# Early-fusion block on one core: selected rows in two image halves, exponential per image with row sums, residual products among the gather

## The chip, the cores and the metric

The kernel runs on one core of one Trainium2 chip. The metric is the device time of one execution in microseconds (us), lower is better. Runs of the kernel before: 225.53 us median of 3 (224.13 to 226.31).

## The reference

Eight images of 3x128x128 are cut into 64 patches each and embedded in 192 channels (first layer `_L0_tok_ref`: feed-forward, window attention, feed-forward). Each image then gets 32 text tokens, so that 96 tokens per image remain. The middle layer is the one that the change touches:

```python
    qkv = (x @ Wqkv_w + Wqkv_b).reshape(b, l, 3, h, hd)          # h = 12 heads of 16
    scores = jnp.einsum('bthd,bshd->bhts', q, k_ * scale)
    attn = jax.nn.softmax(scores + causal_mask, axis=-1)
    ctx = jnp.einsum('bhts,bshd->bthd', attn, v).reshape(b, l, d)
    attn_output = ctx @ out_w + out_b
    selection = jax.nn.softmax((x @ sel_w + sel_b) / temperature, axis=-1)[..., 1:]
    k_sel = int(math.ceil(math.sqrt(l)))                          # 10 of 96
    _, idx = jax.lax.top_k(selection[..., 0], k_sel)
    gated = attn_output * selection
    src = jnp.take_along_axis(gated, idx[..., None], axis=1)
    y = jax.vmap(lambda xb, ib, sb: xb.at[ib].add(sb))(x, idx, src)
```

Only the 10 picked rows of an image are ever used of the attention, so the kernel computes these alone. With `x` the layer-normed tokens, the block's output is `h + y`; a layer norm of it and a feed-forward layer of 16 gated experts and one shared expert follow (`_L0_ffn_ref`), and they take the rest of the time.

## The kernel before, in words

The program is written out by hand for each engine: PE (TensorE), DVE (VectorE), ACT (ScalarE), POOL (GpSimd) and SP, whose queue issues most transfers. Every engine runs its list in order; what one needs of another is a counting semaphore, `wait_ge(s["name"], n)` before and `.then_inc(s["name"], 1)` behind. So the order of the lines within an engine's block is the order of the work, and there is no planner. Sizes: `TOK` = 96 tokens, `PICKED` = 10, `SLOTS` = 80 picked rows of all images, `HALF_IMG` = 4 images in a half, `H2N` = 384 tokens in a half, `CH` = 96 channels (one of two chunks, `ch`), `CHH` = 6 heads in a chunk, `DIM` = 192, `QROWS` = 124 (60 query rows of chunk 0 from row 0, 60 of chunk 1 from row 64). The eight PSUM banks are `bank[0..7]`.

`keep_busy(site, bank)` (L567) issues `FILL[site]` matmuls on constant data whose result nobody reads; the text calls them fillers.

The stage around the change, in the order of the work, for `hf` = 0, 1 (the two halves):

1. DVE picks the ten best of each image (L1667 to L1683), PE sums ranks (L856), and DVE makes the one-hot matrix `hot` (L1690) and `hotp`, weighted by the selection (L1694).
2. Gather: PE opens two banks with the query bias (L862) and adds 16 small products `qv` x `hot` (8 images x 2 chunks, L870) with one filler before every second; DVE spreads each chunk over its heads into `aq_blk` (L1702).
3. PE turns `hotp` (L875), lays the causal mask into the score banks (8 products, L885), then adds 16 score products (L895).
4. Softmax: per half, DVE takes the maximum of each row and image (`amax`, L1493) and subtracts it (L1495), one ACT instruction takes the exponential of 124x384 (L1293), DVE sums (L1500), inverts (L1502) and multiplies (L1504). DVE does both subtractions first, and then sum, inverse and product of half 0, then of half 1.
5. PE turns the probabilities (L909), ACT moves them to SBUF as `aprobT` (L1296), PE multiplies by the values (16 products, `weighted`, L919).
6. DVE keeps each head's own channels: one product of 96x480 with a 0/1 mask into `actx` (L1724) and two sums over the six heads into `ctxT` (L1730), for each half.
7. PE multiplies the bias rows `avb_all` (L942) and the contexts of all 80 picked rows (L945) by `out_w`; DVE adds `out_b` and writes `arow` (L1735).
8. PE adds the picked rows, through `hotpT` (picks, turned, which DVE makes from bank 7 at L1716), to the residual in four `h2_bank`s (8 products, L953). The residual `hx` itself had been put into these banks earlier by 8 products with the identity (`start_h2`, L902).
9. DVE takes statistics of the sum (L1740, L1745), POOL the inverse root (L447, L449), ACT moves the sum to SBUF as `h2` (L1302), DVE normalises into `xn2` (L1603), PE turns it (L785, L786), and the experts follow.

`down_lo(0, 0)` (L1611) splits the first down-projection's weights on DVE; POOL does the same for the first two up-projections (L516) in the same stretch.

Of the kernel before, what the change touches and what calls it, by code (L numbers as in the profile page):

```python
# [19 lines left out]
ALU = mybir.AluOpType  # L20
# [23 lines left out]
SLOTS = IMAGES * PICKED  # L44
# [42 lines left out]
def build(nc, d):  # L87
    with ExitStack() as ctx:
# [9 lines left out]
        h2_bank = [bank[i] for i in (3, 6, 0, 1)]  # L98
# [127 lines left out]
        with ExitStack() as second_life:  # L226
# [25 lines left out]
            hotpT = sb2("hotpT", [SLOTS, IMAGES, TOK])  # L252
# [5 lines left out]
            actx = sb2("actx", [CH, 2, 2 * HALF_IMG, 60])  # L258
            ctxT = sb2("ctxT", [CH, 2, 2, HALF_IMG * PICKED])
            arow = sb2("arow", [SLOTS, DIM])  # L260
# [20 lines left out]
        def v3(ap, n):  # L281
# [243 lines left out]
        def _(pe):  # L525
# [289 lines left out]
            def keys(hf):  # L815
# [31 lines left out]
            tr(bank[2][0:IMAGES, 0:TOK], psel[:, :], c("ident", TOK)[:, 0:TOK]).then_inc(s["psT_ps"], 1)  # L847
            token_rows(7)
            keys(1)
            keep_busy("pickT", bank[3])  # L850
            pe.wait_ge(s["pickT_done"], 1)
            tr(bank[2][0:TOK, 128:128 + IMAGES], pickT[:, :], c("ident", IMAGES)[:, 0:IMAGES])\
                .then_inc(s["pick_ps"], 1)
            keep_busy("pick", bank[3])
            pe.wait_ge(s["pick_done"], 1)
            mm(bank[2][0:TOK, 256:256 + IMAGES], c("tri", TOK), pick[:, :], start=True, stop=True)\  # L856
                .then_inc(s["cum_ps"], 1)

            keep_busy("hot", bank[5])
# [4 lines left out]
            pe.wait_ge(s["hot_done"], 1)  # L864
            for ch in range(2):
                for b in range(IMAGES):
                    if b % 2:
                        keep_busy("gather", bank[2])
# [3 lines left out]
                last.then_inc(s["aq_ps"], 1)  # L872
            pe.wait_ge(s["hot_done"], 2)
            pe.wait_ge(s["av_done"], 8)
            tr(bank[7][0:SLOTS, 256:256 + TOK], hotp[:, :, :].rearrange("p a b -> p (a b)"),  # L875
               c("ident", TOK)[:, 0:TOK]).then_inc(s["hotpT_ps"], 1)
# [10 lines left out]
            keep_busy("aq", bank[5])  # L887
            pe.wait_ge(s["aq_done"], 2)
            for hf in range(2):
                for i in range(HALF_IMG):  # L890
                    b = HALF_IMG * hf + i
                    if i % 2:
                        keep_busy("selected", bank[5])
# [5 lines left out]
            def start_h2(i):  # L899

                for k in range(2):
                    mm(h2_bank[i][0:TOK, DIM * k:DIM * k + DIM], c("ident", TOK)[:, 0:TOK], hx[:, 2 * i + k, :],  # L902
                       start=(k == 0), stop=False, skip_group_check=True)

            def turn_aprob(hf):

                pe.wait_ge(s["as_norm"], hf + 1)
                for i in range(HALF_IMG):
                    last = tr(bank[4 * hf + 1][0:TOK, QROWS * i:QROWS * i + QROWS],  # L909
                              aprob[:, hf, TOK * i:TOK * i + TOK], c("ident", QROWS)[:, 0:QROWS])  # L910
                last.then_inc(s["apT_ps"], 1)
# [11 lines left out]

            pe.wait_ge(s["hx_done"], 2)
            start_h2(0)
            start_h2(1)
            keep_busy("as0", bank[2])
            turn_aprob(0)
            start_h2(2)
            turn_aprob(1)  # L930
            keep_busy("ap0", bank[2])
            weighted(0)
            keep_busy("ap1", bank[4])
            weighted(1)
            start_h2(3)

            pe.wait_ge(s["hotpT_done"], 1)
            keep_busy("ac", bank[7])
            pe.wait_ge(d_aq, 16)
            pe.wait_ge(s["avb_done"], 2)  # L940
            for ch in range(2):
                mm(bank[7][0:SLOTS, 0:DIM], avb_all[:, ch, :], out_w[:, ch, :], start=(ch == 0), stop=False)  # L942
            pe.wait_ge(s["ac_done"], 4)
            for ch in range(2):
                last = mm(bank[7][0:SLOTS, 0:DIM], ctxT[:, ch, :, :], out_w[:, ch, :],  # L945
                          start=False, stop=(ch == 1))
            last.then_inc(s["ao_ps"], 1)

            keep_busy("ao", bank[2])
            pe.wait_ge(s["ao_done"], 1)  # L950
            for i in range(4):
                for k in range(2):
                    last = mm(h2_bank[i][0:TOK, DIM * k:DIM * k + DIM], hotpT[:, 2 * i + k, :],  # L953
                              arow[:, :], start=False, stop=(k == 1), skip_group_check=True)
                last.then_inc(s["h2_ps"], 1)

# [163 lines left out]
        def _(act):  # L1120
# [170 lines left out]
            for hf in range(2):  # L1291
                act.wait_ge(s["as_sub"], hf + 1)
                a(aprob[:, hf, :], aprob[:, hf, :], ACT.Exp).then_inc(s["as_exp"], 1)  # L1293
            for hf in range(2):
                act.wait_ge(s["apT_ps"], hf + 1)
                a(aprobT[:, hf, :], bank[4 * hf + 1][0:TOK, 0:HALF_IMG * QROWS], ACT.Copy)\  # L1296
                    .then_inc(s["apT_done"], 1)

# [99 lines left out]
        def _(dve):  # L1398
# [266 lines left out]
            dve.wait_ge(s["psT_ps"], 1)  # L1665
# [16 lines left out]
            dve.wait_ge(s["pick_ps"], 1)  # L1682
            v.tensor_copy(pick[:, :], bank[2][0:TOK, 128:128 + IMAGES]).then_inc(s["pick_done"], 1)  # L1683

            dve.wait_ge(s["cum_ps"], 1)
# [11 lines left out]

            down_lo(0, 0)
# [7 lines left out]
            for hf in range(2):  # L1706
                b = slice(HALF_IMG * hf, HALF_IMG * hf + HALF_IMG)
                softmax_sub(v3(bank[4 * hf][0:QROWS, 0:H2N], TOK), v3(aprob[:, hf, :], TOK), amax[:, b],
                            QROWS, HALF_IMG, "as_ps", hf + 1, "as_sub")
            for hf in range(2):  # L1710
                b = slice(HALF_IMG * hf, HALF_IMG * hf + HALF_IMG)
                softmax_norm(v3(aprob[:, hf, :], TOK), asum[:, b], arec[:, b], QROWS, HALF_IMG, hf + 1,
                             "as_exp", "as_norm")
            dve.wait_ge(s["hotpT_ps"], 1)
            wide = [SLOTS, IMAGES, TOK]
            v.tensor_tensor(hotpT[:, :, :], bank[7][0:SLOTS, 256:256 + TOK].unsqueeze(1).to_broadcast(wide),  # L1716
                            c("block", SLOTS).unsqueeze(2).to_broadcast(wide), ALU.mult)\
                .then_inc(s["hotpT_done"], 1)

            for hf in range(2):  # L1720
                dve.wait_ge(s["ac_ps"], hf + 1)
                wide = [CH, 2 * HALF_IMG, CHH, PICKED]
                buf = actx[:, hf, :, :]
                k = step(v.tensor_tensor(  # L1724
                    buf.rearrange("p c (h i) -> p c h i", h=CHH),
                    ctx_bank[hf][0:CH, 0:480].rearrange("p (c h i) -> p c h i", c=2 * HALF_IMG, h=CHH),
# [289 lines left out]
```

## Time and profile before

| | us |
|---|---|
| median of 3 runs | 225.53 |
| lowest, highest | 224.13, 226.31 |
| the profiled execution | 226.03 |
| its span, first to last instruction | 224.2 |
| PE busy in the span | 212.6 (95%) |
| DVE busy | 151.0 (67%) |
| ACT busy | 112.9 (50%) |
| POOL busy | 35.3 (16%) |

The profiled execution takes 1.8 us more than its span; that lies before the first and behind the last instruction. Times in rows are us from the span's start. PE's record of a fp32 product is two rows, so "x4" on PE is two products of the program; for transposes and other types it is one. A start on PE, and the length that a matmul shows, overlap with the next one's; how long a row of products takes is read from one start to a later one, or from the chain of work that ended last, which leaves overlaps out. The granted clock is given as a share of full speed: 1.00 is 2.4 GHz, 0.50 is 1.2 GHz.

### The profile page before, as it was taken

Reading aid. Unit: us, or ns where it says so; the run is one execution under the profiler, and the core shown is the slowest. Engines: PE = TensorE matmul, PEld = TensorE weight load, DVE = VectorE, ACT = ScalarE, POOL = GpSimd, SP = SyncE. Lnnn points to the kernel's source line nnn. Section 1 sums busy time; section 2 is a strip of 40 time slices with the busy share of each in tenths; the row PEclk is TensorE's granted clock in tenths of the full one; section 3 lists DMA queues with packets and bytes.
Section 4 is the critical chain, followed back from the end, with each engine's and each line's share of the span. In section 5 each row is a group of like instructions: output and inputs, shape, how many; then the busy total and the mean of one; then the engine's idle time right before and its main releaser. Section 6 shows DMA issues by size and latency. Waiting matters only on the chain.

```text
span 224.2 us, 4277 instructions
## 1 busy us (share of the span) xinstructions
PE 212.6 (95%) x1438; PEld 192.4 (86%) x1438; DVE 151.0 (67%) x406; ACT 112.9 (50%) x227; POOL 35.3 (16%) x61
## 2 busy tenths in 40 slices
PE   6989999999999998999898999999999999999992
PEld 2979998886899986785877897999999999999991
DVE  0168986899204465665769499698878787878763
ACT  2228855557752734431214576266655555555542
POOL 8011003543920524040004000000000000000000
PEclk9999999999999999999999999999999999999999
DMA  6997000000000000021000000655554544544303
GB/s 224 406 394 215 0 1 4 0 3 0 4 0 0 0 3 0 0 61 37 0 3 0 0 18 20 180 154 161 175 140 145 177 141 142 135 135 135 88 0 105
DMA packets 10225, 19.09 MB, mean 85 GB/s; under 512 B 1441, under 2 KB 4657, under 8 KB 10210
## 3 DMA queue, kind: packets, MB, share of 16 engines
q1 hardware_dynamic: 9632, 17.35, 24.7%
q10 hardware_dynamic: 578, 1.54, 1.9%
q8 instruction: 9, 0.15, 0.3%
q14 instruction: 6, 0.05, 0.1%
HBM read 18.25 MB, written 0.64 MB: 84 GB/s over the span
## 4 chain that ended last, share of the span: by engine, by line
PE 76%; DVE 15%; issue 2%; ACT 2%; DMA 2%; POOL 1%; DVEq 0%
PE bank L530 6%; PE bank L532 6%; PE bank L531 6%; PE bank L533 6%; PE bank L534 6%; PE bank L578 4%; PE bank L567 3%; PE bank L1018 3%; PE bank L690 3%; PE bank L1028 2%; PE bank L1019 2%; PE bank L1024 2%; PE bank L1020 2%; PE bank L648 2%; DMA patches<-in_patches 2%
## 5 line engine op out<-in xcount | busy, mean ns | idle before, releaser
L1342 ACT ACTIVATE hid_s<-hid 128x384 fp32r<-128x384 f32 x34 | 17.8, 525 | 28.1 <-DVE hid L1784 27.8
L1332 ACT ACTIVATE silu<-bank,expert_raw 128x384 f32<-128x384 f32 x34 | 19.6, 578 | 9.9 <-PE bank L534 9.7
L1766 DVE SCALAR_TENSOR_TENSOR gated<-bank,expert_raw,silu 128x384 f32<-128x384 f32 x32 | 19.6, 614 | 7.0 <-PE bank L534 6.6
L1790 DVE TENSOR_TENSOR hid_s<-hid,hid_s 128x384 fp32r<-128x384 f32 x34 | 18.6, 553 | 8.4 <-ACT hid_s L1342 8.3
L530 PE MATMUL bank<-tA,ug_w 128*128 128x384 f32 x68 | 23.1, 340 | 0.1
L533 PE MATMUL bank<-tB,ug_w 128*128 128x384 f32 x68 | 22.9, 337 | 0.0
L532 PE MATMUL bank<-tA,ug_w 128*128 128x384 f32 x68 | 22.9, 337 | 0.0
L531 PE MATMUL bank<-tA,ug_w 128*128 128x384 f32 x68 | 22.9, 337 | 0.0
L534 PE MATMUL bank<-tB,ug_w 128*128 128x384 f32 x68 | 22.9, 336 | 0.0
L567 PE MATMUL bank<-filler 128*128 128x512 bf16 x50 | 16.8, 412 | 1.3 <-POOL table L426 1.3
L1784 DVE TENSOR_TENSOR hid<-w_all,gated 128x384 f32<-128x384 f32 x30 | 16.5, 553 | 1.8 <-issue 1.7
L1135 ACT ACTIVATE act<-bank,cols 128x256 f32<-128x256 f32 x24 | 11.1, 473 | 9.0 <-PE bank L552 5.4
L530 PEld LDWEIGHTS bank<-tA,ug_w 128*128 128x128 f32 x68 | 12.8, 188 | 1.1 <-DVE hid L1766 0.4
L534 PEld LDWEIGHTS bank<-tB,ug_w 128*128 128x128 f32 x68 | 12.8, 188 | 0.0
L532 PEld LDWEIGHTS bank<-tA,ug_w 128*128 128x128 f32 x68 | 12.8, 188 | 0.0
L531 PEld LDWEIGHTS bank<-tA,ug_w 128*128 128x128 f32 x68 | 12.8, 188 | 0.0
L533 PEld LDWEIGHTS bank<-tB,ug_w 128*128 128x128 f32 x68 | 12.8, 188 | 0.0
L1018 PE MATMUL bank<-hid_s,dn_w 128*128 128x384 f32 x34 | 11.7, 343 | 0.8 <-issue 0.5
L1019 PE MATMUL bank<-hid_s,dn_w 128*128 128x384 f32 x34 | 11.6, 340 | 0.0
L1020 PE MATMUL bank<-hid_s,dn_w 128*128 128x384 f32 x34 | 11.5, 338 | 0.0
L1024 PE MATMUL bank<-hid_s,dn_w 128*128 128x384 f32 x34 | 11.3, 338 | 0.0
L578 PE MATMUL bank<-patch_w,patches 128*128 128x192 f32 x48 | 10.5, 379 | 0.6 <-DMA patches<-in_patches 0.6
(332 smaller groups left out, 541.5 us busy)
## 6 DMA issues: line engine op xcount, KB each, us to landing
w_all<-routing_weights SPq DMA_DIRECT2D x15, 384.0 KB, 3.7
expert_raw<-in_experts SPq DMA_DIRECT2D x17, 256.0 KB, 3.7
expert_raw<-in_experts SPq DMA_DIRECT2D x17, 97.0 KB, 1.9
patches<-in_patches SPq DMA_DIRECT2D x3, 384.0 KB, 7.4
ff_raw<-in_ff ACTq DMA_DIRECT2D x1, 768.0 KB, 7.4
kv_raw<-in_kv SPq DMA_DIRECT2D x1, 578.0 KB, 11.9
patch_w<-in_patch_w ACTq DMA_DIRECT2D x2, 288.0 KB, 4.0
ff_raw<-in_ff SPq DMA_DIRECT2D x1, 576.0 KB, 8.7
```

The source lines that it names most:

```text
L530: mm(out, wA, aA, start=start, stop=False)
L531: mm(out, wAl, aA, start=False, stop=False)
L532: mm(out, wA, aAl, start=False, stop=False)
L533: mm(out, wBl, aBh, start=False, stop=False)
L534: return mm(out, wB, aB, start=False, stop=True)
L567: mm(out[:, :], filler[:, 0:128], filler[:, :], start=True, stop=True)
L578: mm(bank[4 * (t // 2) + t % 2][:, 0:DIM], patches[:, t, k, :], patch_w[:, k, :], start=(k == 0), stop=False)
L1018: mm(sumA[part], dn_w[p][:, DOWN_HI["A"]], hi, **kw)
L1332: a(silu[hf][:, :], bank[3 + 2 * hf][:, 0:H2N], ACT.Silu, bias=expert_raw[:, p, BU:BU + 1]).then_inc(s[f"silu{hf}"], 1)
L1342: a(hid_s[p][:, 0, H2N * hf:H2N * hf + H2N], hid[hf][:, :], ACT.Copy)\
L1766: v.scalar_tensor_tensor((hid if first else gated)[hf][:, :], bank[4 + 2 * hf][:, 0:H2N], expert_raw[:, p, BG:BG + 1], silu[hf][:, :], ALU ...
L1790: v.tensor_tensor(hid_s[p][:, 1, tok], hid[hf][:, :], f(hid_s[p][:, 0, tok]), ALU.subtract)\
```

## The change

What it does, part by part:

- **Exponential.** The subtraction by DVE (L1495) and the sum by DVE (L1500) are gone. DVE writes the negated maximum of a half; ACT runs four `Exp` of 124x96 per half straight from the score bank, with that maximum as bias and the row sum as second output. DVE keeps inverse and product.
- **Halves.** `hotpT`, `ctxT`, `arow` and the product with `out_w` are made per half (40 picked rows instead of 80). The bias part of that product moves in front of the gather, where DVE makes `brow` of it. A half is finished by adding `brow`.
- **Own heads.** Instead of one 96x480 product and two sums, the two heads that can lie in a group of 32 channels are masked: DVE does channels 32 to 95 in two instructions of 32x160, ACT channels 0 to 31 in two of 32x80, and one DVE addition makes `ctxT`.
- **Residual products.** Four of the eight `start_h2` products stand among the gather, two behind the scores, and two behind the first half's exponential. The banks of `h2_bank` change, and the probabilities are turned into banks 3 and 6.
- **Fillers.** From the pick to the residual there are 11 instead of 27: one in front of the pick's transpose, two in front of the bias products, four in the gather, one in front of the scores, five behind `weighted` and three behind the product with `out_w` are gone.
- **DVE's order.** `hotpT` is made, and `down_lo(0, 0)` done, between `aq_blk` and the maxima.

The diff, cut to its core:

```diff
-        h2_bank = [bank[i] for i in (3, 6, 0, 1)]
+        h2_bank = [bank[i] for i in (1, 5, 7, 0)]
+        turned_bank = (bank[3], bank[6])
...
 # PE
+            for ch in range(2):
+                last = mm(bank[7][0:HSLOTS, 0:DIM], avb_all[:, ch, 0:HSLOTS], out_w[:, ch, :],
+                          start=(ch == 0), stop=(ch == 1))
+            last.then_inc(s["brow_ps"], 1)
...
+            pe.wait_ge(s["hx_done"], 2)
+            pe.wait_ge(s["hot_done"], 1)
+            for ch in range(2):
+                if ch:
+                    pe.wait_ge(s["ak_odd"], 2)
+                gather(ch, range(0, 2))
+                start_h2(1 - ch, 0)
+                gather(ch, range(2, 4))
+                keep_busy("gather", bank[2])
+                gather(ch, range(4, 6))
+                start_h2(1 - ch, 1)
+                gather(ch, range(6, 8)).then_inc(s["aq_ps"], 1)
+                keep_busy("gather", bank[2])
...
+            def attention_rows(hf):
+
+                pe.wait_ge(s["ac_done"], hf + 1)
+                for ch in range(2):
+                    last = mm(turned_bank[hf][0:HSLOTS, 0:DIM], ctxT[:, ch, hf, :], out_w[:, ch, :],
+                              start=(ch == 0), stop=(ch == 1))
+                last.then_inc(s["ao_ps"], 1)
+
+            def picked_rows(hf):
+
+                pe.wait_ge(s["ao_done"], hf + 1)
+                for i in (2 * hf, 2 * hf + 1):
+                    for k in range(2):
+                        last = mm(h2_bank[i][0:TOK, DIM * k:DIM * k + DIM], hotpT[:, 2 * i + k, :],
+                                  arow[:, hf, :], start=False, stop=(k == 1), skip_group_check=True)
+                    last.then_inc(s["h2_ps"], 1)
+
+            start_h2(2, 0)
+            start_h2(2, 1)
+            pe.wait_ge(s["as_exp"], 1)
+            start_h2(3, 0)
+            start_h2(3, 1)
             turn_aprob(0)
-            start_h2(2)
+            pe.wait_ge(s["hotpT_done"], 2)
+            keep_busy("ap0", bank[2])
             turn_aprob(1)
...
             weighted(0)
-            keep_busy("ap1", bank[4])
             weighted(1)
-            start_h2(3)
...
+            attention_rows(0)
+            attention_rows(1)
+            picked_rows(0)
+            picked_rows(1)
 # ACT
             for hf in range(2):
                 act.wait_ge(s["as_sub"], hf + 1)
-                a(aprob[:, hf, :], aprob[:, hf, :], ACT.Exp).then_inc(s["as_exp"], 1)
+                for i in range(HALF_IMG):
+                    tok, b = slice(TOK * i, TOK * i + TOK), HALF_IMG * hf + i
+                    last = a(aprob[:, hf, tok], bank[4 * hf][0:QROWS, tok], ACT.Exp, bias=amax[:, b:b + 1],
+                             accum_out=asum[:, b:b + 1])
+                last.then_inc(s["as_exp"], 1)
...
+            for hf in range(2):
+                act.wait_ge(s["ac_ps"], hf + 1)
+                for par in range(2):
+                    last = a(actx[0:32, hf, :, par, :],
+                             ctx_bank[hf][0:32, 0:480].rearrange("p (c h i) -> p c h i", c=2 * HALF_IMG, h=CHH)[:, :, par, :],
+                             ACT.Copy, scale=c("head", 32)[:, par:par + 1])
+                last.then_inc(s["own_first"], 1)
 # DVE
+            def own_heads(hf):
+
+                dve.wait_ge(s["ac_ps"], hf + 1)
+                wide = [32, 2 * HALF_IMG, 2, PICKED]
+                for g in (1, 2):
...
+                after(k)
+                dve.wait_ge(s["own_first"], hf + 1)
+                two = actx[:, hf, :, :, :].rearrange("p (c b) h i -> p c b h i", c=2)
+                v.tensor_tensor(ctxT[:, :, hf, :].rearrange("p c (b i) -> p c b i", i=PICKED),
+                                two[:, :, :, 0, :], two[:, :, :, 1, :], ALU.add).then_inc(s["ac_done"], 1)
...
+            picks_turned(0)
+            picks_turned(1)
+            down_lo(0, 0)
+            selected_max(0)
+            selected_max(1)
+            selected_norm(0)
+            selected_norm(1)
+            own_heads(0)
+            own_heads(1)
+            dve.wait_ge(s["brow_done"], 1)
+            attention_rows(0)
+            attention_rows(1)
+            last_moments(0)
+            last_moments(1)
```

How the order moves on PE around the gather. In the kernel before, from the ranks' product (`pick`) to the first gather products (`hot`):

```order
L856 MATMUL bank2<-pick,const 96x8 [waits pick_done]
L567 MATMUL bank5<-filler 128x512 x2
L862 MATMUL bank3<-ones,rows 96x80 [waits av_done]
L862 MATMUL bank6<-ones,rows 96x80
L870 MATMUL bank3<-hot,qv 96x10 [waits hot_done]
L567 MATMUL bank2<-filler 128x512
L870 MATMUL bank3<-hot,qv 96x10 x2
L567 MATMUL bank2<-filler 128x512
L870 MATMUL bank3<-hot,qv 96x10 x2
```

In the changed kernel, from the same product to the middle of chunk 0 (`avb_all` is the bias part of the product with `out_w`, `hx` the residual):

```order
L861 MATMUL bank2<-pick,const 96x8 [waits pick_done]
L867 MATMUL bank7<-out_w,avb_all 40x192 [waits avb_done,d_aq]
L867 MATMUL bank7<-out_w,avb_all 40x192
L879 MATMUL bank3<-hot,qv 96x10 [waits hot_done,hx_done]
L879 MATMUL bank3<-hot,qv 96x10
L873 MATMUL bank5<-hx,const 96x192
L879 MATMUL bank3<-hot,qv 96x10 x2
L569 MATMUL bank2<-filler 128x512
L879 MATMUL bank3<-hot,qv 96x10 x2
L873 MATMUL bank5<-hx,const 96x192
```

The bias products moved in front of the ranks' transpose, the fillers behind the ranks' product gave way to the `out_w` products, and every second pair of fillers in the gather to one residual product.

DVE from the maxima to the statistics, before:

```order
L1493 TENSOR_REDUCE amax<-bank 124x4 [waits as_ps]
L1495 TENSOR_TENSOR aprob<-bank,amax 124x384 [waits vec_step]
L1500 TENSOR_REDUCE asum<-aprob 124x4 [waits as_exp]
L1502 RECIPROCAL arec<-asum 124x4 [waits vec_step]
L1504 TENSOR_TENSOR aprob<-aprob,arec 124x384 [waits vec_step]
...
L1716 TENSOR_TENSOR hotpT<-bank,const 80x768 [waits hotpT_ps]
L1724 TENSOR_TENSOR actx<-bank,const 96x480 [waits ac_ps]
L1730 TENSOR_REDUCE ctxT<-actx 96x40 [waits vec_step]
L1730 TENSOR_REDUCE ctxT<-actx 96x40
...
L1735 TENSOR_TENSOR arow<-bank,rows 80x192 [waits ao_ps]
```

DVE in the same place now (`brow` is the bias row, `own_first` ACT's share of the own heads):

```order
L1748 TENSOR_REDUCE amax<-bank 124x4 [waits as_ps] x2
L1756 RECIPROCAL arec<-asum 124x4 [waits as_exp]
L1758 TENSOR_TENSOR aprob<-aprob,arec 124x384 [waits vec_step]
L1756 RECIPROCAL arec<-asum 124x4 [waits as_exp]
L1758 TENSOR_TENSOR aprob<-aprob,arec 124x384 [waits vec_step]
L1767 TENSOR_TENSOR actx<-bank,const 32x160 [waits ac_ps]
L1767 TENSOR_TENSOR actx<-bank,const 32x160
L1775 TENSOR_TENSOR ctxT<-actx 96x2x40 [waits own_first,vec_step]
...
L1781 TENSOR_TENSOR arow<-bank,brow 40x192 [waits ao_ps,brow_done]
L1781 TENSOR_TENSOR arow<-bank,brow 40x192 [waits ao_ps]
```

The two subtractions and two sums are gone, `hotpT` stands earlier, and of the own heads two small products and one addition are left per half.

PE from the last values to the picked rows, before:

```order
L919 MATMUL bank4<-aprobT,qv 96x60 x7
L902 MATMUL bank1<-hx,const 96x192 x2
L567 MATMUL bank7<-filler 128x512 [waits hotpT_done]
L567 MATMUL bank7<-filler 128x512 x4
L942 MATMUL bank7<-out_w,avb_all 80x192 [waits avb_done,d_aq]
L942 MATMUL bank7<-out_w,avb_all 80x192
L945 MATMUL bank7<-out_w,ctxT 80x192 [waits ac_done]
L945 MATMUL bank7<-out_w,ctxT 80x192
L567 MATMUL bank2<-filler 128x512 x3
```

And now:

```order
L939 MATMUL bank4<-aprobT,qv 96x60 x7
L948 MATMUL bank3<-out_w,ctxT 40x192 [waits ac_done]
L948 MATMUL bank3<-out_w,ctxT 40x192
L948 MATMUL bank6<-out_w,ctxT 40x192 [waits ac_done]
L948 MATMUL bank6<-out_w,ctxT 40x192
L957 MATMUL bank1<-arow,hotpT 96x192 [waits ao_done]
```

Between the values and the picked rows there is nothing left but the two halves' products with `out_w`.

## Rows read from the trace of the kernel before

**Rows 1.** Page: busy time by engine, and shares of the chain that ended last.
```profile
PE 212.6 (95%) x1438; PEld 192.4 (86%) x1438; DVE 151.0 (67%) x406; ACT 112.9 (50%) x227; POOL 35.3 (16%) x61
PE 76%; DVE 15%; issue 2%; ACT 2%; DMA 2%; POOL 1%; DVEq 0%
```

**Rows 2.** The chain of work that ended last, 100 to 115 us: start, length, what.
```profile
100.55 0.67 PE bank L567 x3
...
104.61 0.57 DVE amax L1493
...
106.47 0.57 DVE aprob L1504
107.08 0.63 PE bank L909 x4
...
108.97 2.69 PE bank L919 x32
...
112.35 1.08 PE bank L567 x5
...
114.08 0.65 PE bank L945 x4
```

**Rows 3.** Timeline of DVE: start, length, line, idle before with its releaser.
```profile
97.51 1.72 DVE L1611 TENSOR_TENSOR dn_w<-expert_raw,dn_w 128x128 fp32r<-128x128 f32 x2 [1.65 <-ACT dn_w L1290]
...
103.01 0.56 DVE L1493 TENSOR_REDUCE amax<-bank 124x4 f32<-124x384 f32 x1 [2.65 <-PE bank L895]
...
110.34 0.65 DVE L1724 TENSOR_TENSOR actx<-bank,const 96x480 f32<-96x480 f32 x1 [1.19 <-PE bank L919]
...
112.69 1.06 DVE L1730 TENSOR_REDUCE ctxT<-actx 96x40 f32<-96x240 f32 x2
114.77 0.35 DVE L1735 TENSOR_TENSOR arow<-bank,rows 80x192 f32<-80x192 f32 x1 [1.02 <-PE bank L945]
116.11 1.27 DVE L1740 BATCH_NORM_STATS2 st<-bank 96x6 f32<-96x192 f32 x4 [0.98 <-PE bank L953]
```

**Rows 4.** Timeline of PE, from the gather to the picked rows.
```profile
94.96 0.56 PE L862 MATMUL bank<-ones,rows 1*96 1x80 f32 x4
95.45 0.34 PE L870 MATMUL bank<-hot,qv 96*96 96x10 f32 x2
...
99.35 0.26 PE L870 MATMUL bank<-hot,qv 96*96 96x10 f32 x2
...
101.14 0.38 PE L895 MATMUL bank<-akT,aq_blk 96*60 96x96 f32 x4
...
108.34 0.63 PE L909 MATMUL bank<-const,aprob 124*96 124x124 f32 x4
...
115.22 2.80 PE L953 MATMUL bank<-arow,hotpT 80*96 80x192 f32 x16
```

**Rows 5.** Groups of ACT by form, 89 to 128 us: busy, mean ns of one.
```profile
L1264 ACT ACTIVATE qv<-bank 96x384 f32<-96x384 f32 x4 | 1.9, 487 | 1.3 <-PE bank L561 1.3
L1293 ACT ACTIVATE aprob<-aprob 124x384 f32<-124x384 f32 x2 | 1.0, 522 | 7.8 <-DVE aprob L1495 7.8
L1249 ACT ACTIVATE akT<-bank,cols 96x384 f32<-96x384 f32 x1 | 0.6, 576 | 0.4 <-PE bank L534 0.4
L1314 ACT ACTIVATE gexp<-gexp 128x96 f32<-128x96 f32 x1 | 0.3, 283 | 1.2 <-DVE gexp L1810 1.2
```

**Rows 6.** The smallest instruction of ACT (one source line), and of DVE (by form).
```profile
L1188 ACT ACTIVATE table<-table x5: 202/202/203, 4.6 to 129.0; 1x1 f32<-1x1 f32 x5
L1671 DVE MATCH_VALUE_LOAD pT<-top,pT 8x8 f32 x1 | 0.1, 79 | 0.0
```

**Rows 7.** One stretch: busy PE, PEld, DVE, ACT, POOL, then granted clock.
```profile
105.90:107.10 1.20, 0.15 (x2) 0.02 (x1) 1.13 (x4) 0.41 (x1) 0.00 (x0) 1.00 0.00 0
```

**Rows 8.** The patch products, L578: duration ns min/median/max.
```profile
L578 PE MATMUL bank<-patch_w,patches x48: 325/327/660, 4.7 to 17.9; 128*128 128x192 f32 x48
```

**Rows 9.** Timeline of POOL beside the gather.
```profile
96.79 2.36 POOL L516 TENSOR_TENSOR ug_w<-expert_raw,ug_w 128x512 fp32r<-128x512 f32 x2 [8.91 <-ACT ug_w L1260]
```

More of the change, by code:

```diff
@@ L846, in _ @@
             pe.wait_ge(s["psel_done"], 1)
-            tr(bank[2][0:IMAGES, 0:TOK], psel[:, :], c("ident", TOK)[:, 0:TOK]).then_inc(s["psT_ps"], 1)
+            tr(bank[2][0:IMAGES, 0:TOK], psel[:, :], c("ident", TOK)[:, 0:TOK]).then_inc(s["pick_ps"], 1)
             token_rows(7)
             keys(1)
[L850 to L859, printed above, removed]
             pe.wait_ge(s["av_done"], 8)
@@ L886, in _ @@
                    start=(i == 0), stop=False, skip_group_check=True)
-            keep_busy("aq", bank[5])
+            pe.wait_ge(s["brow_done"], 1)
+            keep_busy("aq", bank[7])
             pe.wait_ge(s["aq_done"], 2)
@@ L908, in turn_aprob @@
                 for i in range(HALF_IMG):
-                    last = tr(bank[4 * hf + 1][0:TOK, QROWS * i:QROWS * i + QROWS],
+                    last = tr(turned_bank[hf][0:TOK, QROWS * i:QROWS * i + QROWS],
                               aprob[:, hf, TOK * i:TOK * i + TOK], c("ident", QROWS)[:, 0:QROWS])
@@ L941, in _ @@
[L941 to L955, printed above, removed]
+            attention_rows(0)
@@ L1696, in _ @@
             keys_chunk1(1)
-            down_lo(0, 0)
+            dve.wait_ge(s["brow_ps"], 1)
+            v.tensor_tensor(brow[:, :], bank[7][0:HSLOTS, 0:DIM], row("out_b", 0, HSLOTS), ALU.add)\
+                .then_inc(s["brow_done"], 1)
             wide = [CH, IMAGES, CHH, PICKED]
@@ L1714, in _ @@
-            dve.wait_ge(s["hotpT_ps"], 1)
[L1715 to L1726, printed above, removed]
-                    c("head", CH).unsqueeze(1).unsqueeze(3).to_broadcast(wide), ALU.mult))
-                after(k)
-                for ch in range(2):
-                    v.tensor_reduce(v3(ctxT[:, ch, hf, :], PICKED),
-                                    buf[:, HALF_IMG * ch:HALF_IMG * ch + HALF_IMG, :].rearrange(
-                                        "p c (h i) -> p c i h", h=CHH), AXX, ALU.add)\
-                        .then_inc(s["ac_done"], 1)
@@ L1734, in _, with picks_turned @@
-            dve.wait_ge(s["ao_ps"], 1)
-            v.tensor_tensor(arow[:, :], bank[7][0:SLOTS, 0:DIM], row("out_b", 0, SLOTS), ALU.add)\
-                .then_inc(s["ao_done"], 1)
-            for i in range(4):
-                dve.wait_ge(s["h2_ps"], i + 1)
-                for k in range(2):
-                    k_st = v.bn_stats(st3[:, 2 * i + k, :], h2_bank[i][0:TOK, DIM * k:DIM * k + DIM])
-                k_st.then_inc(s["h2_read"], 1)
-                if i % 2:
-                    dve.wait_ge(s["h2_read"], i + 1)
-                    for b in range(2 * i - 2, 2 * i + 2):
-                        last = v.bn_aggr(mv3[:, b, :], st3[:, b, :])
-                    last.then_inc(s["mv3_done"], 1)
+            def picks_turned(hf):
+                wide = [HSLOTS, HALF_IMG, TOK]
+                v.tensor_tensor(hotpT[:, HALF_IMG * hf:HALF_IMG * hf + HALF_IMG, :],
+                                bank[2][0:HSLOTS, TOK * hf:TOK * hf + TOK].unsqueeze(1).to_broadcast(wide),
+                                c("block", HSLOTS)[:, 0:HALF_IMG].unsqueeze(2).to_broadcast(wide), ALU.mult)\
+                    .then_inc(s["hotpT_done"], 1)
@@ new lines, in attention_rows, with last_moments @@
+            def attention_rows(hf):
+                dve.wait_ge(s["ao_ps"], hf + 1)
+                v.tensor_tensor(arow[:, hf, :], turned_bank[hf][0:HSLOTS, 0:DIM], brow[:, :], ALU.add)\
+                    .then_inc(s["ao_done"], 1)
+            def last_moments(hf):
+                for i in (2 * hf, 2 * hf + 1):
+                    dve.wait_ge(s["h2_ps"], i + 1)
+                    for k in range(2):
+                        k_st = v.bn_stats(st3[:, 2 * i + k, :], h2_bank[i][0:TOK, DIM * k:DIM * k + DIM])
+                    k_st.then_inc(s["h2_read"], 1)
+                dve.wait_ge(s["h2_read"], 2 * hf + 2)
+                for b in range(HALF_IMG * hf, HALF_IMG * hf + HALF_IMG):
+                    last = v.bn_aggr(mv3[:, b, :], st3[:, b, :])
+                last.then_inc(s["mv3_done"], 1)
```

90 lines of the change are left out of this document (50 added, 40 removed), and 4 rows, old and new, of the table FILL.

## The prediction, made before the changed kernel ran

> **What bounds the kernel now.** I read the page first. PE is busy 95% of the span and carries 76% of the chain that ended last [rows 1]. Taken at its word, that says that only less PE work can help. But PE's busy time holds fillers, so the second view is the chain itself in the stage of the change. There DVE stands between pieces of PE: maximum at 104.61, product at 106.47, then the turns at 107.08; and behind the values (108.97) the chain runs through fillers, five of them at 112.35, up to the product with `out_w` [rows 2]. A filler that ends as DVE's result arrives looks like bound work and is a wait. The third view, DVE's timeline, gives the truth of that stretch: the own heads run from 110.34 to 112.69 + 1.06 = 113.75, the bias is added at 114.77, and statistics start at 116.11 [rows 3]. So from the scores on, the stage is a relay: PE, DVE, ACT, DVE, PE, ACT, PE, DVE, PE, DVE. Its length is the sum of the hand-overs, each engine having much idle time. Behind the statistics everything follows by semaphores, and I find nothing there that is tied to the clock on the wall; so what the first statistics (116.11) gain, the end should gain.
>
> **Prices.** Filler: 0.67 / 3 = 0.22 us [rows 2]. Gather product: 15 of them and 8 fillers lie between 95.45 and 99.35 [rows 4], (3.90 - 1.78) / 15 = 0.14. A product with 192 columns: 0.65 / 2 = 0.33 [rows 2]. DVE on PSUM: 0.65 for 480 elements, 0.35 for 192 [rows 3], so 1.04 ns per element and 0.15 fixed: 0.32 for 160, 0.24 for 80, 0.55 for 384.
>
> **1. Up to the scores.** In front of the gather two `out_w` products (0.65) stand where two fillers and two bias products stood. The bias products started at 94.96 [rows 4], the fillers thus at 94.5; 94.5 + 0.65 = 95.15, when `hot` is ready, instead of 95.45. In the gather, 16 products stay (2.25), 4 fillers stay (0.89) and 4 residual products are added (1.3): 4.45 against 16 products and 8 fillers, 4.0. One filler fewer in front of the scores gives 0.22. Sum: -0.3 + 0.45 - 0.22, about -0.1. Bounds: +0.3, if the `out_w` products stall and the shift in front is lost with them, and -0.4, if residual products slip in between weight loads. The new wait for `hx` is free: POOL made it before its 8.91 us of idleness that end at 96.79 [rows 9]. The bias addition on DVE (0.35) and the moved `hotpT` (two of 0.55) and `down_lo` (1.72, beside POOL; less once POOL is done) lie in DVE's idle time before the maxima, 1.65 and 2.65 us [rows 3]: 3.2 of work in 4.3, and PE's scores are not waiting for it. Taken at nothing; if that cover were gone it would cost at most 0.3.
>
> **2. Softmax.** Now: maximum at 103.01, second half turned at 108.34 [rows 3, 4], 5.33 us. In the changed order: maximum 0.56, then eight `Exp` on ACT, then DVE's inverse (by the fixed part 0.16, with hand-overs 0.24) and product (0.61 from 106.47 to the turn at 107.08 [rows 2]). The first four `Exp` wait for the first maximum (103.01 + 0.56 - 0.1 = 103.47), the last four for the second, which comes at 104.61 - 0.1 + 0.57 = 105.08 [rows 2]. Everything hangs on one price that no row shows, an `Exp` of 124x96 with bias and row sum. Without bias and sum it is 0.283; a bias costs 0.576 - 0.487 = 0.09; a source in PSUM rather than SBUF gives 0.035 back (0.487 against 0.522) [rows 5]. For the row sum there must be a read-out: between 0 and ACT's smallest instruction, 0.202; DVE's small helper takes 0.079 [rows 6]. So the ends are 0.28 and 0.58, and I take 0.34 + 0.08 = 0.42. Eight of them: 103.52 + 3.36 = 106.88. With inverse and product, 0.85, the turn comes at 107.73, 0.61 earlier than 108.34. At 0.28 the second maximum becomes the limit (105.1 + 1.1 + 0.85 = 107.0, 1.3 earlier); at 0.58 the turn starts at 109.0, 0.6 later.
>
> The Trainium skill (ScalarE: Activation LUTs, What ACT_TABLE_LOAD costs) gives an ACTIVATE with a bias pointer 280 ns + 0.833 ns per element, and an overlap of 93 ns back to back. By its figures an `Exp` here would take an estimated 0.36, and 0.27 in a row, with nothing said of the row sum; the step would then gain an estimated 1.3 rather than 0.6. This case's row agrees with the slope and the pointer (576 against 487 ns), and no run here yet shows the sum.
>
> **3. Turns, values, own heads.** The turns take 108.97 - 108.34 = 0.63, then 16 value products 2.69 [rows 2, 4], without a break, since ACT moves each half in time. The first half was done at 108.97 + 1.35 = 110.32 and DVE started at 110.34 [rows 3]; the second half is now done at 107.73 + 0.63 + 2.69 = 111.05, and DVE starts at 111.07. DVE per half: two products of 160 elements (0.64), the addition (0.24), hand-over 0.05, so 0.95 instead of 0.65 + 1.06 = 1.7; ACT's two copies of 80 elements, about 0.3 each, run beside them. The last half ends at 112.0. Before, both halves in a row ended at 113.75, DVE being the limit; now PE is, and only the second half's 0.95 lies open. Bounds for one half: 0.8 and 1.5, the latter if ACT and DVE hinder each other.
>
> The two DVE products start at channels 32 and 64. The Trainium skill (VectorE: DVE Perf Modes, Two Vector instructions with no wait between them) says that an instruction whose operands start in another group of 32 partitions than its predecessor's waits until that one has finished. I counted no overlap for them, so this rule costs nothing more than the sum has.
>
> **4. Product with `out_w`, rows, residual.** `out_w` for half 0 runs during own heads 1; for half 1 from 112.08 to 112.73 (before 113.92). Half 0's addition (0.33) runs at 112.04 on DVE, so `arow` 0 is ready at 112.4, and PE goes from one product to the next at 112.73. Before, the addition (114.77 to 115.12) lay open between them: that hand-over of 0.65 is the gain of doing halves. The picked rows' first product thus starts at 112.73 instead of 115.22 [rows 4]: 2.49 earlier. The same 8 products and the same statistics follow.
>
> **Sum.** -0.1 (scores), -0.5 (softmax), -1.1 (values and own heads: 113.75 - 108.34 = 5.4 us become 112.02 - 107.73 = 4.3), -0.1 (PE's start behind them, 0.17 to 0.06), -0.65 (rows by halves): -2.5 us. Against the profiled execution: span 224.2 - 2.5 = 221.7, and with 1.8 around it 223.5. The profiled execution (226.03) is 0.5 above the median of the runs, so the median should be 225.53 - 2.5 = 223.0. A measurement of this kernel can tell about 1% (2.3 us) from no change; the forecast is only just past it.
>
> **Rivals.**
> (a) *Cheap exponential.* If the row sum is free, step 2 gains 1.3 and all of it 3.2: 222.3. For it: the sum would ride on an instruction that passes over the elements anyway. Against: eight instructions stand where two stood.
> (b) *ACT becomes the bound of the softmax.* At 0.58 each the turn is 0.6 late, and the total 1.3: 224.2. For it: ACT's fixed part is large, 0.2 of 0.28 [rows 5, 6], and it is now paid eight times, perhaps sixteen.
> (c) *The gain behind the values is smaller.* Two engines on one bank, small strided instructions and a cross wait bring the own heads to 1.5 per half, then half 1 ends 0.55 later at least, and 0.4 is lost in the gather: 224.0. For it: nothing in this trace runs on 32 channels of a shared bank. Against: PE and not DVE then sets the pace.
> (d) *Slower: PE's clock falls.* 16 fillers fewer leave PE idle for 1.2 us in front of the second turn, and 0.6 in front of the last `out_w` products. If the clock goes to 1.2 GHz there, the following 0.63 + 2.69 + 0.65 + 2.6 = 6.6 us of products take twice that (the same form took 325 and at most 660 ns [rows 8]): +6.6 - 2.5, so 229.6. It decides if the fall comes before the values; a fall behind them costs 3.3 and gives 226.3. Against it: in 105.90 to 107.10 PE was busy 0.15 of 1.2 us, and the granted clock stayed 1.00, 2.4 GHz [rows 7]. [...]
>
> **How the numbers follow.** Forecast 0.45; (a) 0.2; (b) 0.18; (c) 0.12; (d) 0.05. The cases give 222.3 to 224.2 for all but the last; with half a per cent for the measured medians on either side (the three runs lie 2.2 apart) the range is 221.6 to 225.1. Faster by over 1% (below 223.3): (a) whole, and 0.37 of the 0.45 forecast, 0.57. Within 1%: the rest of the forecast, (b) and (c), 0.38. Slower by over 1% (above 227.8): (d), 0.05.
>
> **What would show it right or wrong.** In the changed profile: scores (now L921) starting at 101.0; `Exp` (L1314) rows near 0.34 with a small read-out between them, all eight done by 106.8; the second turn (L929) at 107.7; the addition L1775 of half 1 done at 112.0; L957 at 112.7; statistics at 113.6; the granted clock 1.00 throughout. Exp rows of 0.5 and more, or read-outs of 0.2, would prove (b); own heads over 1.2 us per half (c); 192-column products at 650 ns (d). If the first statistics come at 113.6 and the end has gained less than 2.2, then something behind the stage does not follow the relay, and my reading of the first paragraph is wrong.

## The result: slower by 1.0%, because PE's clock fell

The changed kernel takes 228.47 us (median of 16 executions), the kernel before 225.69 in the same series. The ratio is 1.0097, 95% interval 1.007 to 1.0124. Forecast were 223.0 us, a gain; the measured time lies outside the range. Ratios here leave disturbed executions out on both sides, medians are over all of them; since the granted clock is the matter of this case, it is given for each kernel.

The shares by engine hardly differ. PE's row of granted clock does (page of the changed kernel, one digit per fortieth of the span):

```profile
PE   6989999999999998999899999999999999999992
PEclk9999999999999999999975899999999999999998
```

The slices of 113.5 to 119.1 and 119.1 to 124.8 us are at 7 and 5 tenths. Narrower stretches of the changed kernel (length, busy PE, PEld, DVE, ACT, POOL, then the granted clock):

```profile
114.00:116.00 2.00, 2.00 (x14) 1.97 (x13) 1.47 (x8) 0.69 (x2) 0.00 (x0) 1.00 0.03 8
116.00:118.00 2.00, 2.00 (x10) 1.64 (x9) 1.88 (x12) 1.26 (x3) 1.43 (x4) 0.54 0.00 0
118.00:120.00 2.00, 2.00 (x12) 2.00 (x12) 1.82 (x7) 0.00 (x0) 1.08 (x2) 0.50 0.00 0
124.00:126.00 2.00, 2.00 (x10) 1.28 (x8) 1.11 (x2) 0.86 (x2) 0.00 (x0) 0.50 0.00 0
126.00:128.00 2.00, 1.98 (x14) 1.50 (x12) 0.00 (x0) 0.98 (x2) 0.00 (x0) 0.90 0.00 0
```

TensorE ran at 1.2 GHz for about 10 us, from 116.2 to 126.4, and in the stretch before, 114 to 116, it had been busy for 2.00 of 2.00 us. In all 16 executions the mean granted clock of the span is 0.907 to 0.980; in the 61 of the kernel before that ran beside the experiments it is never under 0.994. The fall is thus no accident of one profile.

How the stage went can be read on DVE, which stands at each hand-over. In the changed kernel (start, length, line, what, idle before and its releaser):

```profile
95.59 0.24 DVE L1724 TENSOR_TENSOR hotp<-hot,psel 96x80 f32<-96x80 f32 x1
...
103.93 0.56 DVE L1748 TENSOR_REDUCE amax<-bank 124x4 f32<-124x384 f32 x1 [1.52 <-PE bank L921]
...
112.50 0.24 DVE L1775 TENSOR_TENSOR ctxT<-actx 96x80 f32<-96x80 f32 x1
112.77 0.35 DVE L1781 TENSOR_TENSOR arow<-bank,brow 40x192 f32<-40x192 f32 x1
113.67 0.35 DVE L1781 TENSOR_TENSOR arow<-bank,brow 40x192 f32<-40x192 f32 x1 [0.56 <-PE bank L948]
114.49 1.27 DVE L1789 BATCH_NORM_STATS2 st<-bank 96x6 f32<-96x192 f32 x4 [0.47 <-PE bank L957]
...
128.80 0.26 DVE L1872 TENSOR_REDUCE gmax<-bank 128x6 f32<-128x96 f32 x1 [3.09 <-PE bank L1008]
```

And two marks of the kernel before that [rows 3] leave out, the first behind the picks and the maximum of the gate's logits, behind the stage:

```profile
95.09 0.24 DVE L1694 TENSOR_TENSOR hotp<-hot,psel 96x80 f32<-96x80 f32 x1
...
126.86 0.26 DVE L1808 TENSOR_REDUCE gmax<-bank 128x6 f32<-128x96 f32 x1 [2.24 <-PE bank L989]
```

The changed profile is 0.5 us late before the stage begins, so only lengths are compared, from mark to mark:

| from, to | before | forecast | changed |
|---|---|---|---|
| picks (`hotp`) to first maximum | 7.92 | 7.8 | 8.34 |
| to the second turn | 5.33 | 4.8 | 4.54 |
| to the first statistics | 7.77 | 5.9 | 6.02 |
| to the gate's maximum | 10.75 | 10.75 | 14.31 |
| sum | 31.77 | 29.3 | 33.21 |

Up to the statistics the stage is 2.1 us shorter; behind them it is 3.6 longer, and most of that stretch ran at half clock. Of the 2.7 us between the two spans (226.9 and 224.2) the stage makes 1.4, the late beginning 0.5 and the part behind the gate's maximum 0.8. The beginning is not the change's: e2, e4 and e5 below have the program of before up to the picks, and their profiles reach `hotp` at 93.48, 93.43 and 93.19 us, where that of before shows 95.09. A median of few executions can be off by as much, so the marks decide here.

PE in the changed kernel (timeline, start and length):

```profile
108.47 0.60 PE L929 MATMUL bank<-const,aprob 124*96 124x124 f32 x4 [1.02 <-DVE aprob L1758]
108.90 2.85 PE L939 MATMUL bank<-aprobT,qv 96*96 96x60 f32 x32
111.69 0.84 PE L948 MATMUL bank<-out_w,ctxT 96*40 96x192 f32 x4
112.79 0.84 PE L948 MATMUL bank<-out_w,ctxT 96*40 96x192 f32 x4 [0.26 <-DVE ctxT L1775]
113.56 2.95 PE L957 MATMUL bank<-arow,hotpT 40*96 40x192 f32 x16
116.44 3.73 PE L983 MATMUL bank<-const,h 96*128 96x96 f32 x16
```

The sizes behind the names say what a product uses of the array: `40*96` is 40 rows by 96 columns. The answering row of before says `80*96` [rows 4]. Both take the same time, 2.8 to 2.95 us, and fill PE's busy share alike. That is a difference that a busy share does not show, and it gave the second theory: not the missing fillers, but products on few rows let the clock fall. It is not the only one of its kind: the products with `out_w` now use 40 columns instead of 80 (`96*40` above). e5 and e6 change only the rows.

### The profile page after: what moved, and what is told of

Same layout as the page of the kernel before. It is cut to its first block, busy times and chain, and to the rows that moved or that the text cites. A ratio compares the mean times of both kernels' runs of the same rounds, so it can differ in the third digit from the quotient of the medians.

```text
span 226.9 us, 4276 instructions
## 1 busy us (share of the span) xinstructions
PE 215.1 (95%) x1427; PEld 195.6 (86%) x1427; DVE 146.8 (65%) x405; ACT 115.7 (51%) x245; POOL 35.3 (16%) x61
## 4 chain that ended last, share of the span: by engine, by line
PE 78%; DVE 13%; issue 3%; ACT 2%; DMA 2%; POOL 1%; DVEq 0%
PE bank L532 6%; PE bank L533 6%; PE bank L534 6%; PE bank L535 6%; PE bank L536 6%; PE bank L580 4%; PE bank L1037 3%; PE bank L983 3%; PE bank L692 3%; PE bank L1047 2%; PE bank L1038 2%; PE bank L1039 2%; PE bank L1043 2%; PE bank L650 2%; DMA patch_w<-in_patch_w 2%
## 5 line engine op out<-in xcount | busy, mean ns | idle before, releaser
L532 PE MATMUL bank<-tA,ug_w 128*128 128x384 f32 x68 | 23.1, 340 | 0.1
L569 PE MATMUL bank<-filler 128*128 128x512 bf16 x34 | 12.0, 426 | 1.3 <-POOL table L428 1.3
```

The source lines that it names most:

```text
L532: mm(out, wA, aA, start=start, stop=False)
```

## The experiments

Each was run beside the kernel before, on the same chip; e1 to e4, e5 to e8 and e9 to e11 ran on three different chips. "Low" counts the executions whose mean granted clock is under 0.985. A dash stands where only one execution was left for a ratio.

| kernel | median us | before | ratio (95%) | low |
|---|---|---|---|---|
| changed kernel | 228.47 | 225.69 | 1.0097 (1.007 to 1.0124) | 16 of 16 |
| e1 wait filled | 226.51 | 225.53 | 1.0046 (1.0007 to 1.0084) | 10 of 10 |
| e2 before, 8 fillers fewer | 229.48 | 225.53 | - | 3 of 4 |
| e3 all waits filled | 226.85 | 225.53 | - | 9 of 10 |
| e4 exponential alone | 223.95 | 225.53 | 0.9944 (0.9904 to 0.9984) | 0 of 10 |
| e5 before, 40 rows | 228.81 | 225.55 | 1.0178 (1.0102 to 1.0253) | 4 of 4 |
| e6 changed, 80 rows | 224.55 | 225.55 | 0.9948 (0.9904 to 0.9991) | 1 of 10 |
| e7 fillers to the end | 224.90 | 225.55 | 0.9969 (0.9932 to 1.0006) | 1 of 10 |
| e8 80 rows and wait | 222.47 | 225.55 | 0.9891 (0.9824 to 0.9957) | 0 of 4 |
| e9, e8 again | 222.22 | 224.97 | 0.9872 (0.9831 to 0.9912) | 0 of 6 |
| e10 residual out of gather | 229.58 | 224.97 | 1.0196 (1.0145 to 1.0247) | 6 of 6 |
| e11 e10 with gather fillers | 223.27 | 224.97 | 0.9921 (0.9885 to 0.9957) | 0 of 12 |

### First round: are the missing fillers the cause?

**e1_wait_filled.** `FILL`: `"ap0": 4`.

> The changed kernel with four fillers in PE's 1.0 us wait in front of the second turn. Theory 1 (the clock falls because PE's waits are no longer filled): granted clock 1.00 throughout, the residual sums take 0.2 us each instead of 0.4, time 2.0 to 2.5 us under the kernel before, about 223.4. Theory 2 (it falls because the picked rows' products now use 40 rows of the array instead of 80, whatever the fillers): the clock is 0.50 from about 116 on as in the changed kernel, time 227 to 228.5.

**e2_before_unfilled.** In the kernel before: `"ac": 0`, `"ao": 0`.

> The kernel before without the eight fillers behind the values (ac 5, ao 3), products still on 80 rows. Theory 1: the clock falls to 0.50 at 112 to 120, time 3 us or more over the kernel before, about 228.7. Theory 2: clock 1.00 throughout, and as the fillers were not on the path, 225.5 to 225.8.

**e3_all_waits_filled.** e1, with `"ac": 2, "ao": 1`, and:

```diff
             attention_rows(0)
+            keep_busy("ac", bank[2])
             attention_rows(1)
+            keep_busy("ao", bank[2])
             picked_rows(0)
```

> The changed kernel with four fillers in front of the second turn, two between the halves' products with out_w and one in front of the picked rows. Theory 1: clock 1.00; if one filled wait was not enough, this one is; the three behind the values cost 0.2 to 0.5 us on the path, time about 223.7. Theory 2: the clock falls, 227.5 to 228.5.

**e4_exponential_alone.** The changed `Exp` on ACT, maximum, inverse and product on DVE, put into the kernel before.

> The kernel before with the new exponential alone (per image, maximum as bias, row sum as second output), all 27 fillers kept. Both theories: clock 1.00. From the first maximum to the second turn 4.5 us as in the changed kernel instead of 5.33, time 0.8 us under the kernel before, about 224.9.

Granted clock on the page of e1, in fortieths of the span:

```profile
PEclk9999999999999999999995999999999999999998
```

On the page of e2:

```profile
PEclk9999999999999999999955899999999999999998
```

On the page of e3:

```profile
PEclk9999999999999999999996799999999999999999
```

And on that of e4:

```profile
PEclk9999999999999999999999999999999999999997
```

e2 speaks for theory 1: eight fillers fewer, nothing else, and the kernel before falls to 1.2 GHz as well, in 3 of 4 executions, after two stretches in which PE was busy 1.38 of 2 us, with waits of 0.79 and 0.45 us for DVE (stretches of e2, columns as above, the granted clock third from the end):

```profile
110.00:112.00 2.00, 1.38 (x9) 1.01 (x7) 1.97 (x4) 0.00 (x0) 0.00 (x0) 1.00 0.00 0
112.00:114.00 2.00, 1.38 (x7) 0.99 (x8) 0.47 (x2) 0.00 (x0) 0.00 (x0) 0.97 0.00 0
114.00:116.00 2.00, 2.00 (x8) 1.78 (x7) 0.63 (x2) 0.49 (x1) 0.00 (x0) 0.50 0.04 8
```

But e1 and e3 speak against it as the whole answer. e1 closes the wait in front of the second turn, e3 nearly all of PE's waits from there to the picked rows, and the clock falls all the same in 19 of 20, only later (at 119.9 instead of 116.2 us in e3's profile). The waits behind the picked rows stay open in both. They are open in the kernel before too, whose PE is busy 1.68 of 2 us there (118 to 120) at a clock of 1.00. The one execution of e3 with a clock of 0.998 took 222.34 us: the relay's gain is there as soon as the clock holds. e4's median is 1.6 us lower, twice the 0.8 that was expected. Its marks show what the exponential gave: 4.45 us from the first maximum to the second turn instead of 5.33, so 0.9; the rest is not in this step, and e4's beginning alone lies 1.7 us before that of the kernel before (93.43 against 95.09).

### Second round: are the 40 rows the cause?

**e5_before_40_rows.** In the kernel before:

```diff
-                    last = mm(h2_bank[i][0:TOK, DIM * k:DIM * k + DIM], hotpT[:, 2 * i + k, :],
-                              arow[:, :], start=False, stop=(k == 1), skip_group_check=True)
+                    last = mm(h2_bank[i][0:TOK, DIM * k:DIM * k + DIM], hotpT[0:40, 2 * i + k, :],
+                              arow[0:40, :], start=False, stop=(k == 1), skip_group_check=True)
```

> The kernel before with all its 27 fillers, but the eight picked-row products use 40 rows of the array instead of 80 (the picked rows of the second half of the images are left out of the sum, nothing else). Theory 1 (fillers alone decide): clock 1.00, time as before, 225.5. Theory 2 (the thin products let the clock fall): clock 0.50 for some 10 us from 116 to 120 on in most executions, 228 to 229.

**e6_after_80_rows.** In the changed kernel `hotpT` and `arow` get 80 partitions, POOL clears them in its idle time, DVE fills rows 0 to 39:

```diff
+            g.memset(hotpT[:, :, :], 0.0).then_inc(s["avb_done"], 1)
+            g.memset(arow[:, :, :], 0.0).then_inc(s["avb_done"], 1)
```

> The changed kernel with no filler added, but the picked-row products on 80 rows again (rows 40 to 79 hold zeros, written by POOL long before). Theory 1: the clock falls as in the changed kernel, mean 0.97, time 227 to 228.5. Theory 2: clock 1.00, and the time is the relay's without the fall, 223.3.

**e7_fillers_to_the_end.** e3, and two fillers each in front of the waits for `h2_done` 4 and `xn2_done` 1.

> The changed kernel with the seven fillers of e3_all_waits_filled and two in each of PE's two waits behind it, for the moved residual and for the normalised rows (0.6 and 0.4 us idle). Theory 1: clock 1.00 in nearly all executions, 223.0 to 223.5, below the kernel before by 2 us or more. Theory 2: clock falls in most executions, 226.5.

**e8_80_rows_and_wait.** e6 with `"ap0": 4`.

> The products on 80 rows and the four fillers in front of the second turn together, 15 fillers in all. Theory 1: still too few behind the values, the clock falls as in e1_wait_filled, 226.5. Theory 2, or both together: clock 1.00, 223.0.

e5 is the kernel before with its 27 fillers. PE's timeline (start, length):

```profile
113.40 2.84 PE L953 MATMUL bank<-arow,hotpT 40*96 40x192 f32 x16
116.17 3.48 PE L964 MATMUL bank<-const,h 96*128 96x96 f32 x16
```

And stretches of e5 around them:

```profile
114.00:116.00 2.00, 2.00 (x14) 1.88 (x12) 1.62 (x9) 0.86 (x2) 0.00 (x0) 1.00 0.04 8
116.00:118.00 2.00, 1.86 (x12) 1.45 (x10) 1.88 (x11) 1.09 (x3) 1.59 (x4) 0.75 0.00 0
118.00:120.00 2.00, 2.00 (x12) 2.00 (x12) 1.82 (x7) 0.00 (x0) 0.92 (x2) 0.50 0.00 0
```

The products take as long as with 80 rows, PE is as busy, and the clock falls in 4 of 4, 1.8% slower. e6 is the way back: the changed kernel, no filler added, the products on 80 rows of which 40 hold only zeros (PE's timeline):

```profile
111.29 2.84 PE L959 MATMUL bank<-arow,hotpT 80*96 80x192 f32 x16
```

Its clock holds in 9 of 10 (the tenth, at 0.91, took 239.26 us, far more than this fall costs), with PE's 1.0 us wait in front of the second turn still open and the `out_w` products still on 40 columns. So it is the rows that a product uses, not the values in them and not its time, that parts the two. Theory 2 has both directions for it. The first is the firmer one, since e5 fell in 4 of 4 beside the kernel before, which held in 19 of 19 on the same chip. The changed kernel itself was not run again on e6's chip. But e8 and e9, which are e1 with 80 rows, held in 10 of 10 on two chips where e1 had fallen in 10 of 10 on a third.

Theory 1 keeps a share: e2 falls at 80 rows, and e7 holds in 9 of 10 at 40 rows once four more fillers stand behind the picked rows. That e3, which lacks only these four, fell in 9 of 10 was seen on another chip, and no run parts the fillers' share from the chip's there. In e6 the 80 rows made good the missing fillers, in e7 enough fillers made good the 40 rows, and in e1 and e3 fewer did not; e8 has neither fault.

### Third round: the better kernel, and the gather

**e9_80_rows_again.** The kernel of e8 in more rounds.

> The same kernel as e8_80_rows_and_wait, timed in more rounds. If the array's rows and the filled wait together hold the clock (theory 2 with theory 1's share): granted clock 0.99 or more in nearly all executions, and the relay's gain of 2.0 to 3.0 us, 222.5 to 223.5 beside 225.5.

The clock on its page:

```profile
PEclk9999999999999999999999999999999999999999
```

222.06 to 222.53 in six executions, ratio 0.9872: with e8 ten of ten hold. The waits behind the picked rows are open here as they are in e1, which differs only in its 40 rows. In the same place PE was about as busy in both, and e1's clock fell at 117.6 us, 23.1 behind its picks (first e1, then e9):

```profile
116.00:118.00 2.00, 1.62 (x13) 1.26 (x12) 1.71 (x9) 0.56 (x2) 1.73 (x4) 0.91 0.00 0
114.00:116.00 2.00, 1.68 (x14) 1.40 (x12) 1.88 (x10) 1.05 (x3) 1.64 (x4) 1.00 0.00 0
```

Marks of e9 on DVE:

```profile
93.44 0.24 DVE L1726 TENSOR_TENSOR hotp<-hot,psel 96x80 f32<-96x80 f32 x1
...
101.77 0.56 DVE L1750 TENSOR_REDUCE amax<-bank 124x4 f32<-124x384 f32 x1 [1.52 <-PE bank L923]
...
112.28 1.01 DVE L1791 BATCH_NORM_STATS2 st<-bank 96x6 f32<-96x192 f32 x3 [0.47 <-PE bank L959]
...
123.03 0.26 DVE L1874 TENSOR_REDUCE gmax<-bank 128x6 f32<-128x96 f32 x1 [2.23 <-PE bank L1010]
```

8.33, 10.51 and 10.75: 29.6 in all, against 31.8 before and 29.3 forecast. The last stretch is exactly that of before. The 3.56 us of the changed kernel were the clock's. Between the two profiles the stage gained 2.2 us; the 2.75 between the medians has 0.6 more than the stage explains.

**e10_residual_out_of_gather.** e8 without the two `start_h2` lines in the gather, `for i in (0, 1, 2): start_h2(i, 0); start_h2(i, 1)` behind the scores, `"ap0": 1`.

> e8 with the four residual products taken out of the gather and put behind the scores, and one filler instead of four in front of the second turn. In the changed kernel a residual product costs 0.46 in the gather, not the 0.33 that was forecast. If that is on the path: scores start 1.8 us earlier, PE's work behind them (8 products, 2.6 us, and the first turn) just fits in the 3.1 us to the second turn, time 1.0 to 1.8 us under e8, about 221. If the maxima or the exponential were what holds the stage, nothing is gained, 222.5. If four fillers in the gather are too few without the residual products: clock 0.97, 225.

**e11_gather_fillers_back.** e10 with a filler in the place of each residual product in the gather.

> e10 with eight fillers in the gather as in the kernel before. Clock 0.99 or more in all cases; scores 0.9 us later than in e10, about 222, which is e10's time plus 0.9 if the gather is on the path, and the same if it is not.

In e10 the clock falls much earlier, at 97.4 us, just behind the gather. That runs from 93.7 to 97.1, and PE is without a pause in it (stretches of e10):

```profile
94.00:96.00 2.00, 2.00 (x25) 1.89 (x24) 1.10 (x3) 1.89 (x5) 0.80 (x1) 1.00 0.02 4
96.00:98.00 2.00, 2.00 (x20) 1.83 (x19) 0.98 (x3) 0.00 (x0) 1.52 (x2) 0.86 0.31 50
98.00:100.00 2.00, 1.75 (x10) 1.17 (x10) 1.02 (x4) 0.00 (x0) 0.00 (x0) 0.50 0.68 209
```

The gather before the change had eight fillers; the changed kernel keeps four and has a residual product in the place of each of the others. Each of the 16 gather products is two passes on PE. With 32 passes of ten columns and four fillers it fell in 6 of 6; with eight fillers (e11) it held in 12 of 12, and with four fillers and four residual products (e8, e9) in 10 of 10. e11's first maximum comes 7.67 us behind the picks instead of 8.33, yet its first statistics 18.75 instead of 18.84: PE now has eight residual products in front of the turns, which wait there for PE and no longer for DVE. Nothing is gained: up to the gate's maximum it is 29.5 us behind the picks, 29.6 in e9. The median is 1.0 us over e9's, which the stage does not explain.

## Why the prediction was wrong

**The reading of the bound was right.** "A filler that ends as DVE's result arrives looks like bound work and is a wait": 2.12 us were gained up to the statistics (2.5 forecast) although PE's share stayed at 95%, and in e9, where the clock holds, the stage's 2.2 us reach the end (2.75 between the medians).

**Step 1, scores: missed, -0.1 forecast, +0.4 measured.** The gather began 0.15 earlier (0.3 forecast), but lasted 4.73 (95.80 to 100.53) instead of 4.45: a residual product costs (4.73 - 2.25 - 0.89) / 4 = 0.40 among small products, not 0.33. That is just outside the bound given (+0.3).

**Step 2, exponential: right way, too dear.** ACT's timeline of the changed kernel (start, length):

```profile
104.52 0.34 ACT L1314 ACTIVATE aprob<-bank,amax 124x96 f32<-124x96 f32 x1 [6.54 <-DVE amax L1748]
104.76 0.19 ACT L1314 ACTIVATION_READ_ACCUMULATOR aprob<-bank,amax 124x1 f32 x1
104.85 0.33 ACT L1314 ACTIVATE aprob<-bank,amax 124x96 f32<-124x96 f32 x1
105.08 0.20 ACT L1314 ACTIVATION_READ_ACCUMULATOR aprob<-bank,amax 124x1 f32 x1
```

The `Exp` is 0.34 as forecast, the read-out 0.20, the upper bound; but they overlap by 0.1 at each seam, so one pair takes 105.17 - 104.85 = 0.32, not 0.42. That is the condition of rival (a): the second half's `Exp` start behind its maximum, at 106.12, and not right behind those of the first. The step gained 0.79 instead of 0.5, of the 1.3 that (a) gave it. The Trainium skill (ScalarE: Activation LUTs, What ACT_TABLE_LOAD costs) gives an overlap of 93 ns for ACTIVATEs back to back; this trace agrees (0.09 to 0.10, here between an `Exp` and a read-out), and with it the sum would have been nearer.

**Steps 3 and 4: right.** From the second turn to the end of the own heads 4.27 us (4.29 forecast), from there to the picked rows 0.82 (0.71 forecast). The two products on other partitions did not overlap: two of 0.32 took 0.67. The Trainium skill (VectorE: DVE Perf Modes, Two Vector instructions with no wait between them) had said so. Rival (c) is out.

**The step that failed is the picked rows' products, "the same 8 products", whose change was put at nothing, and with it the 0.05 for rival (d).** The clock fell, as (d) has it, but not where (d) puts it. (d) has it fall at PE's waits and slow the products with `out_w` and the picked rows: "a fall behind them costs 3.3 and gives 226.3". Measured, those products ran at full clock (2.95 us for the picked rows against 2.80), the fall came as the last of them ended, at 116.2, and what it slowed were the residual sums, the turns and the gate, by 3.56. That 3.3 and 3.56 are near each other is luck, and the time was 228.47, 2.2 over the 226.3. The argument against (d) failed: "in 105.90 to 107.10 PE was busy 0.15 of 1.2 us, and the granted clock stayed 1.00". That gap was followed in the kernel before by fillers and by products on 96 and 80 rows; the same gap in e6 did no harm either. I counted idle time alone. The change also halved the rows of eight products on the path. e5 shows that halving them alone loses 1.8%: its PE was busy 2.00 of 2.00 us in every stretch from 106 to 116, and the clock fell at 117.0. In e2 idle time did count, 0.79 and 0.45 us just before the fall, at 80 rows. The Trainium skill (TensorE: Matmul & The Clock Gate, HAM oscillation — how this bites in real kernels) tells of a clock that falls in waits for DMA between bursts. Those waits are longer than any in this stage, and the falls of e5 and e10, with PE busy, are not among what it tells.

The range is also a little narrower than its own half per cent makes it (221.2 to 225.3, not 221.6 to 225.1); nothing hangs on that.

**What stays open.** The changed kernel's part behind the gate's maximum is 98.1 us against 97.3 before; e9 has 97.4. The 0.7 us lie in the loop over the experts and were not looked into; e1 has 98.2 there and e3 97.5, and both fell. So the distance from 226.3 to 228.47 is known only in part. That the rows make the difference was shown for 40 against 80 in one place; other sizes were not tried. Why rows count and not PE's busy time, no run shows.

## What to carry to other kernels

Before fillers are taken out or a product is cut into thinner ones, look at what PE does in the same stretch: a PE that was always busy, but on few rows (e5) or with very short products (e10), lost its clock here, and rows are free (80 rows, 40 of them zeros, take the 2.84 us that 40 take). Judge such a change by the granted clock over many executions, and by lengths between marks, not by the total alone. Here the shorter relay alone loses 1.0%; with the clock kept it gains 1.3% (e9), of which the stage's 2.2 us are 1.0%.

## What the runs showed of the hardware that I had not expected

Of two kernels whose PE is equally busy, the one with products of 40 rows falls to 1.2 GHz in 4 of 4 executions (e5) and the one with 80 never did in 61. Once fallen, the clock stayed low for 10.2 us in the changed kernel although PE was busy 2.00 of 2.00 us the whole time, with transposes, 96-column products and, from 124.1 us on, the gate's products of 384 columns. And PE at full busy share, with a gather of ten-column products in which one pass in nine is a filler, falls as well (e10).
